# An attention layer with a router: the product with the values one unit later, output rows per batch

## The reference

```python
h = gelu(x[:, 1:] @ W1 + x[:, :1] @ W2 + b)                  # 16 x 255 rows
z = layernorm(h)
q, k, v = split_heads(z @ Wq.T), ...                         # 16 heads of 64
p = exp(s - max(s)); p = p / (sum(p) + 1e-10)                # s = q k^T / 8
h = h + (p @ v) @ Wo.T + bo
z2 = layernorm(h)
probs = softmax(z2 @ router_w); two best of 8 experts per row
h = h + sum of two experts(z2) + sigmoid(z2 @ gate_w) * shared(z2)
```

## Time and profile before

| | us |
|---|---|
| median of 3 runs | 1192.36 |
| lowest, highest | 1192.11, 1195.31 |
| the profiled execution | 1195.21 |
| its span (first to last instruction) | 1193.4 |
| TensorE busy in it | 1070.7 |
| VectorE, ScalarE, GpSimd busy | 814.0, 691.3, 389.8 |

### The profile page before, as it was taken

The page is one execution under the profiler, slowest core; times in us unless marked ns, Lnnn a source line. Parts: engine busy times, 40 slices in busy tenths (PEclk is TensorE's granted clock), DMA queues, the critical chain, the costliest instruction groups (busy, mean ns, idle before and its releaser), DMA issues. The chain is left out here.

```text
span 1193.4 us, 26027 instructions
## 1 busy us (share of the span) xinstructions
PE 1070.7 (90%) x8010; PEld 881.0 (74%) x8011; DVE 814.0 (68%) x2254; ACT 691.3 (58%) x2156; POOL 389.8 (33%) x452
## 2 busy tenths in 40 slices
PE   7979899999999999999999999999976079999897
PEld 6857677768777776777777687777755079999786
DVE  3757767784886688588767858866772456666466
ACT  4647656773775576377647647765761055555454
POOL 0021212242224223322412332241232258745455
PEclk9989999999999999999999999999998589999999
DMA  7110000000001000000000000000001275444564
GB/s 247 54 41 1 1 2 18 2 20 19 18 0 36 18 0 9 27 18 0 36 18 0 9 27 18 0 36 19 2 14 40 73 244 166 134 136 129 193 229 141
DMA packets 46596, 65.56 MB, mean 55 GB/s; under 512 B 7992, under 2 KB 39608, under 8 KB 45496
## 3 DMA queue, kind: packets, MB, share of 16 engines
q1 hardware_dynamic: 36472, 41.48, 11.2%
q0 software_dynamic: 6528, 17.97, 4.2%
q10 hardware_dynamic: 3520, 5.25, 1.4%
HBM read 36.22 MB, written 28.46 MB: 54 GB/s over the span
## 5 line engine op out<-in xcount | busy, mean ns | idle before, releaser
L723 ACT ACTIVATE prob<-s_ps,nmax 128x255 f32<-128x255 f32 x512 | 240.1, 482 | 275.0 <-DVE nmax L836 273.3
L1111 POOL TENSOR_SCALAR prob<-prob,rinv 128x255 f32<-128x255 f32 x128 | 126.6, 989 | 584.9 <-DVE rinv L855 584.9
L836 DVE TENSOR_REDUCE nmax<-s_ps 128x2 f32<-128x510 f32 x256 | 164.8, 674 | 19.0 <-issue 9.4
L581 PE MATMUL o_ps<-probT,v 128*64 128x256 f32 x1024 | 139.8, 392 | 41.6 <-ACT probT L748 39.9
L581 PEld LDWEIGHTS o_ps<-probT,v 128*64 128x64 f32 x1024 | 69.8, 136 | 104.1 <-ACT v L744 58.9
L568 PE MATMUL pT_ps<-ident,prob 128*128 128x128 f32 x1024 | 135.4, 276 | 0.9 <-DVE prob L858 0.9
L568 PEld LDWEIGHTS pT_ps<-ident,prob 128*128 128x128 f32 x1024 | 117.0, 142 | 2.9 <-DVE prob L858 1.8
L858 DVE TENSOR_SCALAR prob<-prob,rinv 128x255 f32<-128x255 f32 x256 | 107.0, 460 | 4.6
L723 ACT ACTIVATION_READ_ACCUMULATOR prob<-s_ps,nmax 128x1 f32 x512 | 108.8, 213 | 0.0
L864 DVE COPY probT<-pT_ps 128x512 f32<-128x512 f32 x128 | 87.0, 680 | 14.9 <-PE pT_ps L568 14.2
L67 PE MATMUL v_ps<-wv_hi,zT_lo 128*128 128x256 f32 x256 | 86.6, 338 | 0.9 <-ACT v L744 0.9
(11 more groups left out here) (253 smaller groups left out, 3007.2 us busy)
## 6 DMA issues: line engine op xcount, KB each, us to landing
xg<-expert_in_rows SPq DMA_DIRECT2D x72, 130.0 KB, 2.2
up_space<-expert_out_rows SPq DMA_DIRECT2D x8, 1024.0 KB, 5.0
xin<-in_x_dram SPq DMA_DIRECT2D x8, 512.0 KB, 4.6
z_rows<-z SPq DMA_DIRECT2D x8, 512.0 KB, 3.2
z<-z_rows ACTq DMA_DIRECT2D x7, 512.0 KB, 3.5
out_dram<-resid SPq DMA_DIRECT2D x8, 256.0 KB, 3.4
out_dram<-resid SPq DMA_DIRECT2D x8, 224.0 KB, 3.3
expert_in_rows<-bo_row SPq DMA_DIRECT2D x12, 128.0 KB
```

The source lines that it names most:

```text
L581: m = pe.matmul(o_ps[h * DH:(h + 1) * DH, 0:N], vt[:, 2 * b + kt, col:col + DH], probT[u_par(i)][:, h, kt, :], start=kt == 0, stop=kt == 1)
L723: m = act.activation(prob[u_par(i)][:, h, qt, 1:N], s_ps[h][:, qt * N + 1:(qt + 1) * N], ACT.Exp, bias=nmax[u_par(i)][:, n:n + 1], accum_o ...
L836: dve.tensor_reduce(nmax[u_par(i)][:, 2 * h:2 * h + 2], s_ps[h][:].rearrange("p (q k) -> p q k", q=2)[:, :, 1:N], AX_X, ALU.max, negate=Tr ...
L1111: pool.tensor_scalar(prob[k][:, 1, 0, 1:N], prob[k][:, 1, 0, 1:N], rinv[k][:, 2:3], None, ALU.mult).then_inc(s_nB, 1)
```

## The change

`values(g, i)` is no longer issued in unit i, but in unit i+1 behind the scores of unit i+2; the last one of a group is issued in unit 0 of the next. The stages of a unit on TensorE are now scores, values of the unit before, transposes, q or k, v, router step. ScalarE and VectorE follow: `o_hi` of the unit before stands between the two halves of the exponentials, `probT_a` behind them, `v_copy` at the end of the unit; `o_lo` of the unit before stands behind `probT_b` and ahead of the router rows.

`output_rows` and `add_rows` take a half j. Half 0 (batch 0) ends the group as before; half 1 is issued at the end of unit 0 of the next group. In the last group, values of unit 15 stand between the two halves.

Router steps come one unit later, except that the best two and the one-hot rows now share unit 10, the rank matmuls come ahead of the transposes in unit 11, and their copy out of PSUM is in `places`. The eight indirect DMAs of a group stand in units 13 to 15 as two, three and three.

```diff
-            def output_rows(g, last):
-                for j in range(2):
-                    pe.wait_ge(s_ol, UNITS * g + UNITS - 1 + j + FREE_B)
-                    pe.wait_ge(s_qkl, UNITS * g + UNITS + (-1 if last else 3) + j)
...
+            def output_rows(g, j, last):
+                pe.wait_ge(s_ol, UNITS * g + UNITS - 1 + j + FREE_B)
+                pe.wait_ge(s_qkl, UNITS * g + UNITS + (-1 if last else 3) + j)
...
-                if i in (3, 4):
-                    c = i - 3
+                if i in (4, 5):
+                    c = i - 4
...
                         m = pe.transpose(ps[:, t * P:(t + 1) * P], z2[:, t, c * P:(c + 1) * P], ident[:])
                     m.then_inc(s_zt2, 1)
-                elif i == 5:
...
                     m.then_inc(s_lg, 1)
-                elif i == 10:
+                elif i == 11:
 
                     pe.wait_ge(s_taken, r + 1)
                     idle_bank(g, i)
...
                     ahead = i + 4
                     if i == UNITS - 4 and not last:
+                        if not first:
+                            router_bank_read(g, i)
                         transpose_z(g + 1, True)
                     if i + 1 < UNITS:
                         scores(g, i + 1, True)
...
                     def next_v():
                         if ahead < UNITS or not last:
                             pe.wait_ge(s_ve, UNITS * g + ahead)
-                            if i == UNITS - 4:
-                                pe.wait_ge(s_zl, DC * (g + 2))
                             project_v(g + ahead // UNITS, ahead % UNITS)
 
-                    if i != UNITS - 4:
-                        next_v()
+                    if i > 0:
+                        values(g, i - 1)
+                    elif not first:
+                        values(g - 1, UNITS - 1)
+                    if i == 11 and not first:
+                        router_step(g, i)
                     transpose_p(g, i)
-                    if i == UNITS - 4:
-                        next_v()
                     next_qk()
-                    values(g, i)
+                    next_v()
                     if not first:
-                        router_step(g, i)
-                output_rows(g, last)
+                        if i != 11:
+                            router_step(g, i)
+                        if i == 0:
+                            output_rows(g - 1, 1, False)
+                output_rows(g, 0, last)
+                if last:
+                    values(g, UNITS - 1)
+                    output_rows(g, 1, last)
 
             transpose_z(0, False)
...
                         exps(*nxt, 0)
-                    if has_tile and i != UNITS - 4:
-                        v_copy(*tile)
-                    probT_a(g, i)
-                    if has_tile and i == UNITS - 4:
-                        v_copy(*tile)
+                    if i > 0:
+                        o_hi(g, i - 1)
+                    elif not first:
+                        o_hi(g - 1, UNITS - 1)
                     if has_next:
                         exps(*nxt, 1)
+                    probT_a(g, i)
                     if has_tile:
                         qk_hi(*tile)
                     if has_next:
                         normalise_b1(*nxt)
-                    o_hi(g, i)
+                    if has_tile:
+                        v_copy(*tile)
                     if not first:
                         router_step(g, i)
+                if last:
+                    o_hi(g, UNITS - 1)
 
             z_hi(0)
             act.wait_ge(s_mask, 2)
                 dve.tensor_tensor(oT_lo[:, i // 2, part], o_ps[:, 0:N], f32(oT_hi[:, i // 2, part]),
                                   ALU.subtract).then_inc(s_ol, 1)
...
-                                      ALU.add).then_inc(s_woe, 1)
+            def add_rows(g, j):
...
 
             def places(r):
                 after(dve.tensor_copy(run[:, 0, :], run[:, GT, :]), s_chain2, PLACE_STEPS, r, 1)
+                dve.wait_ge(s_rank, r + 1)
+                dve.tensor_copy(ranks[:].rearrange("p a t e -> p (a t e)"), proj_ps[0][:, 0:2 * GT * E]).then_inc(s_rank_read, 1)
                 dve.wait_ge(s_rank_read, r + 1)
                 for t in range(GT):
...
                     dve.wait_ge(s_lr, r + 1)
                     dve.tensor_reduce(row_nmax[:], logits[:, :, 0:E], AX_X, ALU.max, negate=True).then_inc(s_nm, 1)
-                elif i == 11:
-                    dve.wait_ge(s_rank, r + 1)
-                    dve.tensor_copy(ranks[:].rearrange("p a t e -> p (a t e)"), ps[:, 0:2 * GT * E]).then_inc(s_rank_read, 1)
 
...
                 r = g - 1
-                if i in (0, 1):
-                    dve.wait_ge(s_woe, 2 * r + i + 1 + FREE_W)
-                    for t in (2 * i, 2 * i + 1):
+                if i in (1, 2):
+                    tiles = (2 * i - 2, 2 * i - 1)
+                    dve.wait_ge(s_woe, 2 * r + i + FREE_W)
+                    dve.sem_inc(s_go, 1)
+                    for t in tiles:
...
                         dve.sem_inc(s_go, 1)
                         dve.bn_aggr(mean_var2[:, t, :], stats2[:, t, :]).then_inc(s_mv2, 1)
-                elif i == 2:
...
-                elif 8 <= i < 13:
-                    (probabilities, best_two, one_hot, places, row_slots)[i - 8](r)
+                elif i == 9:
+                    probabilities(r)
+                elif i == 10:
+                    best_two(r)
+                    one_hot(r)
+                elif i == 11:
+                    places(r)
+                elif i == 12:
+                    row_slots(r)
...
                         maxima(*nxt, 1)
                     probT_b(g, i)
+                    if i > 0:
+                        o_lo(g, i - 1)
+                    elif not first:
+                        o_lo(g - 1, UNITS - 1)
                     if not first:
                         router_rows(g, i)
                     if not last and 3 <= i < 3 + GT:
                         normalise_a(*nxt)
                     if has_tile:
                         qk_lo(*tile)
-                    o_lo(g, i)
-                add_rows(g)
+                    if i == 0 and not first:
+                        add_rows(g - 1, 1)
+                add_rows(g, 0)
+                if last:
+                    o_lo(g, UNITS - 1)
+                    add_rows(g, 1)
 
...
-                elif i >= UNITS - GT:
-                    t = i - (UNITS - GT)
-                    if t == 0:
+                elif i > UNITS - GT:
+                    if i == UNITS - GT + 1:
                         pool.wait_ge(s_marked, r + 1)
                         pool.wait_ge(s_slot, r + 1)
                         pool.sem_inc(s_pgo, 1)
-                    for n in range(TOP):
+                    for t, n in ((0, 0), (0, 1), (1, 0), (1, 1), (2, 0), (2, 1), (3, 0), (3, 1))[
+                            {13: slice(0, 2), 14: slice(2, 5), 15: slice(5, 8)}[i]]:
                         pool.indirect_dma_start(
                             x_slots, bass.IndirectOffsetOnAxis(ap=slot_now[:, t, n:n + 1], axis=0),
                             z2_twice[:, n, t, :], None).then_inc(s_scat, 16)
```

64 lines of the change are left out of this document (34 added, 30 removed).

## The result

| | kernel before | changed kernel |
|---|---|---|
| median, us | 1192.82 (4 runs) | 1203.84 (4 runs) |
| lowest, highest | 1192.11, 1195.31 | 1203.50, 1207.52 |
| ratio to before | 1 | 1.0096, interval 1.0071 to 1.012 |
| the profiled execution, its span | 1195.21, 1193.4 | 1203.80, 1202.0 |
| mean granted clock | 0.965 | 0.949 |

I forecast 1175.8 us and gave a slower kernel 7%. It became slower by 11 us: 28 us more than forecast.

A forecast was written before the change was run, and what follows sets the result against it. TensorE, busy 90% of the span, was held back by waits, mostly for probT from the VectorE-ScalarE ring. Losses of 53.6 us before less 37.0 left gave 16.6: 1192.4 to 1175.8 us, range for 8 in 10 1164 to 1188.

The forecast's parts named there:

- The ordinary unit: Attention unit without router work: waits for probT go, TensorE becomes the bound, 5.09 us instead of 5.60.
- Ring: VectorE and ScalarE handing over to each other within one unit: falls from 5.53 to 4.81 us.
- The rival of dear borders between stages: TensorE's three new stage borders per unit each cost 0.1 more, 38 us: 1214 us; chance 6%.
- Group 0: First group, no router: start wait 2.0, clock 1.5, z transposes' wait 0.35; 3.9 us left.
- The border of groups: Starts of groups 2 to 5, behind VectorE's jump: TensorE waits 0.7 for oT_lo, no clock loss; 2.8 us left.
- The clump: Router steps in groups 1 to 6: waits of 2.0 and 2.2, 4.7 per group, 28.2 us left.
- The rival of a cheaper clump: Router steps in groups 1 to 6 lose 2.6, not 4.2, per group; 10 us more gain, 1166; chance 13%.
- The clump's clock: Half clock behind the router waits: taken as 0; as rival 1.5 per group, 9 us, 1185; chance 15%.
- the sign that I had named for the rival: A fall of the granted clock in unit 12 of each group, for the 15% rival of 9 us.
- Scatters: Rival: three indirect DMAs in units 14 and 15 delay GpSimd's normalising, 7 us, 1183; chance 3%.
- The sum: Whole kernel: 53.6 us lost before less 37.0 left, gain 16.6, forecast median 1175.8 us.

The follow-up runs named there:

- e1_after_shift60: Changed kernel with sixty counting instructions on TensorE near the program's start, ahead of its attention loop; 1178.49 us, ratio 0.9873.
- e7_after_flat_spread: Changed kernel with all four attention loops written out and VectorE's router steps spread over more units; 1177.89 us, ratio 0.9714.
- e8_after_flat_end: Changed kernel with all four attention loops written out and both output-row halves again at each group's end; 1191.07 us, ratio 0.9825.
- e12_after_flat_late: Changed kernel with all four attention loops written out and router steps still later, one-hot in unit 12, places in 14; 1151.11 us, ratio 0.9636.
- e10_after_pe_flat: Changed kernel with only TensorE's attention loop written out; 1173.44 us, ratio 0.9831.
- e9_after_free60: Changed kernel with sixty counting instructions ahead of TensorE's attention loop, placed where TensorE waits anyway; 1175.00 us, ratio 0.9832.
- e4_after_flat: Changed kernel with the attention loops written out on TensorE, ScalarE, VectorE and GpSimd; 1160.04 us, ratio 0.9711.

## Why the prediction was wrong, point by point

**The ordinary unit: right.** Ring below TensorE's own time, units of 5.05 us (5.09 forecast), waits for probT gone. The rival of dear borders between stages is refuted: the three new borders cost nothing. That units take 5.05 and not 5.09 is worth about 0.04 x 128 = 5 us (an estimate) that the sum did not have.

**Group 0: right in its waits.** They are 2.16 at the start and 0.38 at the z transposes, as forecast 2.0 and 0.35. The 1.5 of half clock behind the first did not come in this trace (the next unit takes 5.05); in those of `e1_after_shift60`, `e7_after_flat_spread`, `e8_after_flat_end` and `e12_after_flat_late` it did (6.62 to 6.66).

**The border of groups: the step that failed.** I followed VectorE's jump and what it delays, and that came exactly: with TensorE's loop written out, output rows wait for oT_lo six times,

```profile
PE proj_ps L67 <- DVE oT_lo L882: 4.9, 6, 1.1
```

of which 2.1 are the two at the tail, so 4 x 0.7 = 2.8, the number of the sum. But I gave TensorE's own jump no line of its own. The sentence "VectorE's loop jumps back" had no counterpart for TensorE, although the change moved instructions from ahead of its loop into it, and although two rows of before bore on that: a branch of 0.2 us, and an instruction queue that was silent while the loop turned, hence code that was held, by a margin that I did not look at. The missing term is 32 us by the ratios: 5 x 4.0 of idle, and most of the rest half clock at the same five borders.

**The clump: right in size and place.** The rival of a cheaper clump (2.6 per group) did not come. Forecast 4.7 per group with waits of 2.0 and 2.2; in `e10_after_pe_flat` one group shows 1.74 and 2.27 (TensorE's timeline):

```profile
443.80 0.18 PE L625 MATMUL proj_ps<-taken,before 128*128 128x32 bf16 x1 [1.74 <-DVE q_lo L855]
...
449.79 0.66 PE L521 MATMUL proj_ps<-ident,z 128*128 128x128 f32 x4 [2.27 <-DVE k_lo L855]
```

**The clump's clock: wrong in the changed kernel.** I took 0 and made 9 us a rival. In the changed kernel the granted clock falls at the z transposes or in the unit behind them in groups 1 and 3 to 6, the sign that I had named for the rival. The unit behind them in group 3, by windows:

```profile
459.74:465.90 6.16, 6.16 (x41) 4.78 (x40) 3.67 (x11) 3.89 (x12) 0.00 (x0) 0.80 0.01 3
```

In groups 3 to 6 these units take 6.17, 7.49, 6.59 and 6.67 us for 5.05, 6.7 us together. After the same two waits other traces show such a stretch in some groups and not in others: `e9_after_free60` has one in each of groups 1 to 5, 9.2 us together (units of 6.04 to 7.58 for 5.05); `e10_after_pe_flat` in groups 1 and 6 alone, 3.1. One of those in `e9_after_free60`, by windows:

```profile
453.85:459.89 6.04, 6.04 (x43) 4.75 (x42) 3.68 (x11) 3.89 (x12) 0.00 (x0) 0.81 0.00 0
```

TensorE never waits in it and takes 6.04 for 5.05. What decides whether it comes stays open; two nearly equal kernels differ in it.

**Scatters: refuted.** On GpSimd they take 959/974/1232 ns as before (that is the instruction; in the changed kernel the transfer lands 2.6 us after its issue at the median), and no wait of the transposes for GpSimd appears.

**The sum.** The forecast is that of the change without the refetch: 1175.8. The two kernels that have only that taken away measured 1175.00 and 1173.44 beside a kernel before of 1194.43, a gain of 20.2 against the forecast 16.6. That they lie so close is in part luck: by the traces, whose executions differ with the half clock, the phase is 19.7 us shorter in the one (`e9_after_free60`) and 26.7 in the other. The change as it stands has the refetch, though, and neither the range nor a rival allowed for it. A slower kernel had 7%, but for dear borders of stages (1214 us), which the units of 5.05 refute; that it did become slower does not speak for that rival.

## What to carry to other kernels

For each engine with a hardware loop that the change lengthens, shortens or shifts, note whether its instruction queue is silent while the loop turns; if so its code is held, and one asks by how many instructions it may move before it is not. The cheapest trial of such a loss is some tens of idle instructions ahead of the loop (sixty here); the cure is to write the loop out. And a stall in a kernel before may be free only because another engine's stall lies over it: a change that removes the second one bares the first, so both are to be listed.

## What was not expected of the hardware

- TensorE's jump back over 6.5 packets of code takes 0.2 us if they are still held and 3.3 to 3.9 if not. Then a second stop follows: 2.3 to 2.5 us where the next packet's border comes 44 records behind the jump, 0.4 to 0.9 where it comes 85 behind.
- VectorE's jump costs 2.33 us in the changed kernel's order too, where TensorE no longer waits for its maxima there (VectorE's timeline of `e10_after_pe_flat`):

```profile
377.38 1.29 DVE L848 TENSOR_REDUCE nmax<-s_ps 128x2 f32<-128x510 f32 x2 [2.33 <-issue]
```

- A written out program of the same work is faster than its loop even where no jump is waited for: the stretch with the z transposes takes 9.57 in `e4_after_flat`, and in `e10_after_pe_flat` 10.31 to 10.35 in groups 1 to 5 and 9.53 in group 6, which VectorE has written out in both. In a loop VectorE has 353 records a group, 111 of them on registers and 23 on semaphores; written out it has 232, none on registers and 14 on semaphores. That these make the difference was not tried alone.
